# One layer of spiking attention and a mixture of experts: projections' inputs in four buffers, VectorE's work in a new order, biases in the first weight row, late weight pieces spread evenly

## The chip, the cores and the metric

The kernel runs on one core of a Trainium2 chip. The metric is device time in microseconds for one execution of the program. Five engines work side by side, each through its own instruction queue, and wait for each other on semaphores: TensorE (PE in the profile; its weight loads are PEld), VectorE (DVE), ScalarE (ACT), GpSimd (POOL) and SyncE (SP, which only issues DMAs). A DMA whose rows go to computed addresses (DMA_INDIRECT) is issued by GpSimd, one instruction for 128 rows.

## What is computed

The input x is (2, 2048, 256) float32, 4096 tokens. Cut to what matters:

```python
xn = (x - mean(x)) / sqrt(var(x) + 1e-5)                     # over the 256 features
Q, K, V = (spike(layer_norm(xn @ W.T + b) * g + beta - 1.0) for W, b, g, beta in q, k, v)
attn = Dh - hamming(Q, K) + log_pe_bias(N, N)                # 16 heads of 16; no softmax
out  = spike((attn * scale) @ V - 0.5)
out  = spike(layer_norm(out @ Wo.T + bo) * go + betao - 1.0)
gate = the two largest of softmax(xn @ router.T), scaled to sum 1    # 8 experts
moe  = sum over the two experts of gate * ((silu(h[:, :256]) * h[:, 256:]) @ down), h = xn @ up
result = x + out + moe
```

`spike(v)` is 1 where v >= 0, else 0. Since there is no softmax, attention is done as linear attention: a 16x16 sum of K-by-V products per head, and the position bias apart.

## The kernel before

**Tiles and stages.** Tokens go in 32 tiles of 128 (NT), tile t being block t // 2 of batch t % 2. Five stages follow each other, with engines overlapping at the seams.

1. *Start (0 to 49 us).* SyncE loads x in five chunks (`X_CHUNKS`), ScalarE's queue loads the four projection weights `w_f` and small tables. VectorE takes statistics (L760), GpSimd the power -1/2 (`first_rstd`, L648), VectorE normalises each tile in place (L782). TensorE transposes tiles (L1122), ScalarE copies them to `xT` (`keep_xT`), and TensorE forms the router's logits from them (L1134). The projection weights are centred over their output features and given the sign of the gain: ScalarE sums them (`sum_weights`, L418), VectorE subtracts and multiplies (L803). The biases take the same way on two partitions (L424, L807, L435, L813) into `bias_r`. ScalarE then rounds the weights to the fp32r type (`w_h`, L430) and VectorE keeps the rest (`w_l`, L818).
2. *Routing (50 to 65 us).* VectorE picks the two experts of each token and computes each row's slot, ending in `pos` (L896, semaphore `placed`). A second part, `rest_of_routing`, gives the slots of the padding rows (`pads_placed`) and the expert of each slot tile (`owner`).
3. *Projections (49 to 165 us).* For each tile ScalarE writes the rounded `xT_h` (`keep_xh`, L441) and VectorE the rest `xT_l` (`keep_xl`, L790), both in **two** buffers, so that tile t's must wait for the projections of tile t-2. TensorE computes Q, K and V of tile t: for each, one matmul of ones by `bias_r` (L1180), then for each of two chunks of features three products, high by high, high by low, low by high (L1102 to L1104). The results of two tiles (a pair) fill six half banks of PSUM; there are two such sets. ScalarE sums squares (`squares`, L494), takes the root (L500); VectorE refines it (`deviations`, L938 to L944), compares (`spikes`, L955), which frees the banks. TensorE turns Q of tile t-4 before tile t (L1168, one bank, emptied by ScalarE's `keep_qT`, L482), and adds K by V of tile t-4 after it (L1189). In the same stage the 24 pieces of expert weights are split into two fp32r parts: the first 8 by ScalarE and GpSimd (L453, L653), 16 later ones by ScalarE and VectorE (L453, L932), one for every second tile up to tile 19, then one a tile up to tile 27 (`late_piece`). Also in this stage GpSimd scatters the normalised rows to their slots in HBM (`slot_x`): 64 scatters of tiles (L672) and 7 of padding rows (L679, two behind each tile from tile 3 on). They start at `placed`; tile t's wait for all projections of tile t+2 (`proj_done` >= 3(t + LEAD)).
4. *Experts (175 to 373 us).* For each of 71 slot tiles: load `ex` from `slot_x`, transpose, up-projection, SiLU times the other half, transpose, down-projection, scatter to `slot_y`. SyncE issues the first load only when all 71 scatters have landed and all weight pieces are split (L349 to L351).
5. *Output (373 to 451 us).* Attention, output projection, gating, sums, store.

**What sets the order.** There is no planner: each engine's queue holds its instructions in the order in which its block of the code writes them, all 32 tiles written out. ScalarE's turn for tile t is: `keep_qT(t-4)`, `keep_xh(t+1)`, a late piece, then the squares. VectorE's is: `keep_xl(t+1)`; for even t `deviations` and three spikes of the pair before, for odd t its other three; then a late piece.

## Time and profile before

| | us |
|---|---|
| median of 3 runs | 454.08 (453.01 to 455.45) |
| the profiled execution, its own time | 452.64 |
| its span, first to last instruction | 450.8 |
| busy: TensorE / VectorE / ScalarE / GpSimd | 383.5 / 273.9 / 232.0 / 215.8 |
| mean granted TensorE clock | 0.941 of full speed |

A row of the timeline gives the start in us, the time in us, engine, line, operation, what is written and read, the count, and in brackets how long the engine was idle before it and who ended that. Where several like instructions stand in one row they overlap in the pipeline, so the distance between starts, not the mean time, is the price of one. A row of groups gives the busy time and the mean in ns, then the idle time before these instructions and its releasers. Idle time of an engine that is not the bottleneck costs nothing.

### The profile page before, as it was taken

What the parts mean: (1) busy time and instruction counts of PE and PEld (TensorE: products, weight loads), DVE (VectorE), ACT (ScalarE), POOL (GpSimd) and SP (SyncE); (2) the same over time, 40 slices, a digit from 0 to 9 for tenths busy, and PEclk for the clock granted to TensorE, in tenths of its full rate; (3) what the DMA queues carried; (4) which work ended last, traced back from release to release, by engine and by line L of the source; (5) the groups of instructions that cost most, each with busy time, mean ns of one, the idle gap of its engine ahead of it and who ended that gap; (6) DMA issues with size and microseconds to landing.
All of it is one profiled execution on the core that took longest, in us unless ns stands there. A gap on an engine that the chain in (4) does not pass through costs nothing.

```text
span 450.8 us, 8962 instructions
## 1 busy us (share of the span) xinstructions
PE 383.5 (85%) x2525; PEld 311.6 (69%) x2526; DVE 273.9 (61%) x774; ACT 232.0 (51%) x752; POOL 215.8 (48%) x213
## 2 busy tenths in 40 slices
PE   5489768688989944999999999999999998999860
PEld 1223758578988843788888888888888875666650
DVE  5799998346878733445444555445444534479984
ACT  1466745447687742444544545454545434566650
POOL 5252447666677671133333333333333332489983
PEclk9699889889999985899999999999999999999966
DMA  8752113334445322254443434343434323982222
GB/s 259 246 164 71 47 60 105 120 117 131 130 133 185 107 94 84 64 186 121 140 124 120 125 117 128 117 126 118 125 120 122 92 77 100 386 320 95 94 72 93
DMA packets 40434, 59.01 MB, mean 131 GB/s; under 512 B 6294, under 2 KB 27926, under 8 KB 40408
## 3 DMA queue, kind: packets, MB, share of 16 engines
q1 hardware_dynamic: 31712, 38.53, 28.5%
q0 software_dynamic: 6848, 18.70, 11.4%
q10 hardware_dynamic: 1848, 1.47, 1.1%
q8 instruction: 13, 0.21, 0.2%
q14 instruction: 13, 0.11, 0.1%
HBM read 35.79 MB, written 22.89 MB: 130 GB/s over the span
## 4 chain that ended last, share of the span: by engine, by line
PE 57%; DVE 12%; POOL 10%; issue 9%; ACT 5%; DMA 4%; SPq 1%; another core or an unknown queue 0%; POOLq 0%; DVEq 0%; ACTq 0%
PE bank L1104 15%; PE bank L1102 15%; PE bank L1103 14%; POOL xres L713 4%; PE bank L1228 3%; PE bank L1244 3%; POOL xres L706 3%; DMA xn<-x 3%; PE bank L1180 2%; DVE xn L782 2%; ACT junk L494 2%; DVE xst L760 2%; POOL slot_x L672 1%; POOL rstd L698 1%; DVE xT_l L790 1%
## 5 line engine op out<-in xcount | busy, mean ns | idle before, releaser
L687 POOL DMA_INDIRECT slot_y<-ey,dest x71 | 68.6, 966 | 138.2 <-ACT ey L547 108.4
L672 POOL DMA_INDIRECT slot_x<-xn,pos x64 | 66.4, 1038 | 34.9 <-PE bank L1104 15.2
L990 DVE TENSOR_TENSOR hid<-gact,bank 128x256 f32<-128x256 f32 x71 | 29.9, 421 | 78.2 <-ACT gact L531 52.4
L1102 PE MATMUL bank<-ew,exT_h 128*128 x142 | 63.6, 448 | 5.3 <-issue 4.5
L531 ACT ACTIVATE gact<-bank 128x256 f32<-128x256 f32 x71 | 27.4, 386 | 65.7 <-PE bank L1104 65.7
L1104 PE MATMUL bank<-ew,exT_l 128*128 x142 | 56.8, 400 | 0.0
L1103 PE MATMUL bank<-ew,exT_h 128*128 x142 | 56.8, 400 | 0.0
L1103 PE MATMUL bank<-w_l,xT_h 128*128 128x256 f32 x192 | 55.6, 290 | 1.3 <-issue 1.3
L1104 PE MATMUL bank<-w_h,xT_l 128*128 128x256 f32 x192 | 55.6, 290 | 0.2 <-issue 0.2
L1102 PE MATMUL bank<-w_h,xT_h 128*128 128x256 f32 x192 | 55.5, 289 | 0.1
L494 ACT ACTIVATE junk<-bank 128x256 bf16<-128x256 f32 x96 | 35.8, 384 | 37.2 <-PE bank L1104 37.2
L1102 PE MATMUL bank<-ew,hidT_h 128*128 x142 | 45.6, 321 | 1.0 <-DVE hidT_l L994 1.0
L541 ACT ACTIVATE hidT_h<-bank 128x256 fp32r<-128x256 f32 x71 | 27.3, 385 | 33.0 <-issue 23.0
L994 DVE TENSOR_TENSOR hidT_l<-bank,hidT_h 128x256 fp32r<-128x256 f32 x71 | 30.1, 424 | 21.0 <-ACT hidT_h L541 21.0
L1103 PE MATMUL bank<-ew,hidT_h 128*128 x142 | 39.9, 281 | 0.0
L1104 PE MATMUL bank<-ew,hidT_l 128*128 x142 | 39.9, 281 | 0.0
L1103 PEld LDWEIGHTS bank<-w_l,xT_h 128*128 128x128 f32 x192 | 38.2, 199 | 2.0 <-issue 2.0
L1180 PE MATMUL bank<-bias_r,ones_r 128*128 128x256 f32 x96 | 30.6, 318 | 10.2 <-DVE v_spk L955 4.9
L1102 PEld LDWEIGHTS bank<-w_h,xT_h 128*128 128x128 f32 x192 | 38.6, 201 | 0.0
L1104 PEld LDWEIGHTS bank<-w_h,xT_l 128*128 128x128 f32 x192 | 38.3, 199 | 0.4 <-issue 0.4
L924 DVE TENSOR_TENSOR exT_l<-bank,exT_h 128x256 fp32r<-128x256 f32 x71 | 29.6, 417 | 13.6 <-ACT exT_h L536 13.5
L1228 PE MATMUL bank<-id_f,ex 128*128 128x128 f32 x142 | 27.9, 280 | 9.6 <-DMA ex<-slot_x 9.5
(193 smaller groups left out, 960.9 us busy)
## 6 DMA issues: line engine op xcount, KB each, us to landing
ex<-slot_x SPq DMA_DIRECT2D x71, 129.0 KB
y_tok<-slot_y SPq DMA_DIRECT2D x8, 1024.0 KB, 13.9
ew_f<-experts SPq DMA_DIRECT2D x24, 256.0 KB
xres<-x SPq DMA_DIRECT2D x16, 256.0 KB
out<-xres SPq DMA_DIRECT2D x16, 256.0 KB, 2.1
xn<-x SPq DMA_DIRECT2D x6, 512.0 KB, 11.7
slot_y<-ey,dest POOLq DMA_INDIRECT x71, 2.4
xn<-x SPq DMA_DIRECT2D x4, 256.0 KB, 3.9
```

The costliest lines, as they stand in the source:

```text
L494: nc.scalar.activation(junk[:, i, :], proj_ps[r][i], ACT.Square, accum_out=ssq[:, r, i:i + 1]).then_inc(s["ssq_done"], 1)
L531: nc.scalar.activation(gact[:, m % 2, :], h_ps[m % 2][:, 0:F], ACT.Silu).then_inc(s["gact_done"], 1)
L672: pool.indirect_dma_start(slot_x, bass.IndirectOffsetOnAxis(ap=pos[:, k, t:t + 1], axis=0), xn[:, t, :], None).then_inc(s["scattered"], 16)
L687: pool.indirect_dma_start(slot_y, bass.IndirectOffsetOnAxis(ap=dest[:, m % 4:m % 4 + 1], axis=0), ey[:, m % 4, :], None).then_inc(y_out[m ...
L924: v.tensor_tensor(flat2(exT_l[:, m % 2, :, :]), ex_ps[m % 2], flat2(exT_h[:, m % 2, :, :]).bitcast(F32), ALU.subtract).then_inc(s["exl_set ...
L990: v.tensor_tensor(hid[:, m % 2, :], gact[:, m % 2, :], h_ps[m % 2][:, F:2 * F], ALU.mult).then_inc(s["hid_done"], 1)
L994: v.tensor_tensor(flat2(hidT_l[:, m % 2, :, :]), hT_ps[m % 2], flat2(hidT_h[:, m % 2, :, :]).bitcast(F32), ALU.subtract).then_inc(s["hidl_ ...
L1102: mm(dst, a_h, b_h, start=first, stop=False)
L1103: mm(dst, a_h, b_l, start=False, stop=False)
L1104: return mm(dst, a_l, b_h, start=False, stop=last)
L1180: mm(proj_ps[r][i], ones_r[:, :], bias_r[:, cols], start=True, stop=False)
L1228: last = turn(ex_ps[m % 2][:, c * P:(c + 1) * P], ex[:, u, c * P:(c + 1) * P], id_f[:, :])
```

## The change

**Biases.** A normalised row sums to zero over its 256 features, so subtracting the first row of a weight matrix from all its rows leaves the product as it is and makes the first row zero. The host now puts the biases of Q, K and V into that first row and passes the old one as `w_first`. The kernel loads it to all partitions (`w0_r`, 128 times 3 KB), GpSimd subtracts it from both chunks of `w_f` (`subtract_base`) and sets the first feature of every tile in `xT` to 1.0 after the router has read it (`set_ones`). The bias matmul L1180 goes from the projections (`bias_r` remains for the output projection alone, so the four bias steps work on a quarter of the data, or run once in place of four times). ScalarE's `sum_weights` moves behind its first two copies of `xT`, since it needs the subtracted weights.

**Buffers and order.** `xT_h` and `xT_l` have four buffers (`RING`). ScalarE's turn for tile t becomes: two squares first, then `keep_qT(t-4)`, `keep_xh(t+3)`, a late piece; for odd t the last two squares, the root and `keep_xh(t+3)` come behind. VectorE goes by pairs: `deviations`, `keep_xl`, four spikes, `keep_xl`, two spikes, then late pieces; `rest_of_routing` stands behind pair 1. TensorE waits for spikes bank by bank instead of once a tile.

**Late pieces.** The 16 late pieces go to tiles 5, 6, 8, 10, 11, 13, ... 28, 30, three to five tiles. Waits for piece buffers that hold older data are put at the piece concerned.

The diff, without renamed arguments and without the waits just named:

```diff
--- before.py
+++ after.py
+RING = 4
 ...
-        bias_r = keep("bias_r", [P, G4 * D], F32R)
+        bias_r = keep("bias_r", [P, D], F32R)
 ...
+        w0_r = place_in(r_a + KC * G3 * D * 4)("w0_r", [P, G3 * D])
 ...
-        xT_h = put("xT_h", [P, 2, KC, P], F32R)
-        xT_l = put("xT_l", [P, 2, KC, P], F32R)
+        xT_h = put("xT_h", [P, RING, KC, P], F32R)
+        xT_l = put("xT_l", [P, RING, KC, P], F32R)
 ...
-        def late_piece(m, i):
-            if m < 8 + LOOP and m % 2 == 0:
-                return None
-            n = POOL_PIECES + (m - PIECE_STEP) // 2 if m < 8 + LOOP else POOL_PIECES + (8 + LOOP - PIECE_STEP) // 2 + m - 8 - LOOP + 1
-            return (n + (0 if i is None else i * 2), n) if m >= PIECE_STEP and n < PIECES else None
+        LATE_PIECES = {PIECE_STEP + (n - POOL_PIECES) * 5 // 3: n for n in range(POOL_PIECES, PIECES)}
 ...
             act.dma_start(w_f[:, :, :], w_all.rearrange("(c k) n -> k c n", k=P)).then_inc(s["w_in"], 16)
+            act.dma_start(w0_r[:, :], w_first.partition_broadcast(P)).then_inc(s["base_in"], 16)
 ...
-                act.wait_ge(s["b_signed"], G4)
+                act.wait_ge(s["b_signed"], 1)
 ...
-            def keep_xh(t, m=None):
-                m = t if m is None else m
-                if not early(t, 2):
-                    act.wait_ge(s["proj_done"], G3 * (t - 1))
-                nc.scalar.activation(flat2(xT_h[:, m % 2, :, :]), xT_of(t), ACT.Copy).then_inc(s["xh_set"], 1)
 ...
-            act.wait_ge(s["w_in"], 16)
-            for n in range(KC * G4):
-                sum_weights(n)
             for g in range(NT // RG):
                 keep_xT(2 * g)
                 keep_xT(2 * g + 1)
+                if g == 0:
+                    act.wait_ge(s["w_based"], KC)
+                    for n in range(KC * G4):
+                        sum_weights(n)
 ...
-            def project(t, m, i):
-                if not early(t, 4):
-                    keep_qT(t - 4, m - 4)
-                if not (num(t) and t >= NT - 1):
-                    keep_xh(t + 1, m + 1)
-                late = late_piece(m, i)
-                if m == 11:
-                    act.wait_ge(s["bias_set"], 1)
-                    act.wait_ge(s["pads_done"], 16 * PC)
-                if late:
-                    piece_upper(late[0], late[1], i)
-                if m == 0:
-                    nc.scalar.activation(rstd[:, 0, 0:1], eps_c[:, 0:1], ACT.Sqrt)
-                if early(t, 4):
+            def project(t):
+                even = t % 2 == 0
+                if even:
+                    act.wait_ge(s["b_summed"] if t == 0 else s["ssq_done"], 1 if t == 0 else G3 * t)
+                act.wait_ge(s["proj_done"], G3 * t + (2 if even else 1))
+                squares(t, 0 if even else 2)
+                if t >= 4:
+                    keep_qT(t - 4, t - 4)
+                if even and t + 3 < NT:
+                    keep_xh(t + 3)
+                if t in LATE_PIECES:
+                    piece_upper(LATE_PIECES[t])
+                if t < 4:
                     for n in ((4, 5), (), (6, 7), ())[t]:
-                        piece_upper(n, n)
-                squares(t, m)
-                if m % 2 == 1:
-                    deviations(t, m)
+                        piece_upper(n)
+                if not even:
+                    act.wait_ge(s["proj_done"], G3 * t + 3)
+                    squares(t, 4)
+                    deviations(t)
+                    if t + 3 < NT:
+                        keep_xh(t + 3)
             act.wait_ge(s["eps_set"], 1)
             act.wait_ge(s["xT_ready"], NT // 2)
-            steps(project)
+            nc.scalar.activation(rstd[:, 0, 0:1], eps_c[:, 0:1], ACT.Sqrt)
+            keep_xh(1)
+            keep_xh(2)
+            for t in range(NT):
+                project(t)
 ...
-            for c in range(len(X_CHUNKS) - 1):
+            def subtract_base(c):
+                g.tensor_tensor(w_f[:, c, 0:G3 * D], w_f[:, c, 0:G3 * D], w0_r[:, :], ALU.subtract).then_inc(s["w_based"], 1)
+            def set_ones(group):
+                pool.wait_ge(s["logitsT"], group + 1)
+                n = RG if (group + 1) * RG <= XT_TILES else RG // 2
+                for t in range(0, RG, n):
+                    where, at = xT_part(group * RG + t)
+                    last = g.memset(where[0:1, at:at + n, 0, :], 1.0)
+                last.then_inc(s["ones_in"], 1)
+            first_rstd(0)
+            first_rstd(1)
+            pool.wait_ge(s["w_in"], 16)
+            pool.wait_ge(s["base_in"], 16)
+            subtract_base(1)
+            pool.wait_ge(s["w_based"], 1)
+            g.memset(w0_r[0:1, :], 0.0).then_inc(s["row0_gone"], 1)
+            pool.wait_ge(s["row0_gone"], 1)
+            subtract_base(0)
+            for c in range(2, len(X_CHUNKS) - 1):
                 first_rstd(c)
             piece_lower(0, 0)
             first_rstd(len(X_CHUNKS) - 1)
             for n in range(1, POOL_PIECES):
+                if n < 4:
+                    set_ones(n - 1)
                 if n == 4:
+                    for group in range(3, NT // RG):
+                        set_ones(group)
                     pool.wait_ge(s["w_halved"], 2 * KC)
                     g.tensor_tensor(wo_l[:, :, :], w_f[:, :, G3 * D:], wo_h[:, :, :].bitcast(F32), ALU.subtract).then_inc(s["wo_parted"], 1)
                 piece_lower(n, n)
 ...
-            def keep_xl(t, m):
+            def keep_xl(t):
                 dve.wait_ge(s["xh_set"], t + 1)
-                if not early(t, 2):
-                    dve.wait_ge(s["proj_done"], G3 * (t - 1))
-                v.tensor_tensor(flat2(xT_l[:, m % 2, :, :]), xT_of(t), flat2(xT_h[:, m % 2, :, :]).bitcast(F32),
+                if t >= RING:
+                    dve.wait_ge(s["proj_done"], G3 * (t - RING + 1))
+                v.tensor_tensor(flat2(xT_l[:, t % RING, :, :]), xT_of(t), flat2(xT_h[:, t % RING, :, :]).bitcast(F32),
                                 ALU.subtract).then_inc(s["xl_set"], 1)
 ...
-            for g in range(G4):
-                cols = bias_f[:, g * D:(g + 1) * D]
-                v.scalar_tensor_tensor(cols, cols, b_mean[:, 1, g:g + 1], sgn_r[0:2, g * D:(g + 1) * D],
-                                       ALU.subtract, ALU.mult).then_inc(s["b_signed"], 1)
-            keep_xl(0, 0)
+            v.scalar_tensor_tensor(bias_f[:, :], bias_f[:, :], b_mean[:, 1, 0:1], sgn_r[0:2, G3 * D:],
+                                   ALU.subtract, ALU.mult).then_inc(s["b_signed"], 1)
+            keep_xl(0)
 ...
-            def project(t, m, i):
-                pair = (t // 2 if num(t) else i * 2 + m // 2) - 1
-                if not (num(t) and t >= NT - 1):
-                    keep_xl(t + 1, m + 1)
-                if m % 2 == 0:
-                    deviations(t - 2, m - 2, pair)
-                    spikes(t - 2, m - 2, 0)
-                else:
-                    spikes(t - 3, m - 3, 1)
-                late = late_piece(m, i)
-                if late:
-                    piece_lower(*late)
+            def project(pair):
+                deviations(pair)
+                keep_xl(2 * pair + 4)
+                spikes(pair, 0, 4)
+                keep_xl(2 * pair + 5)
+                spikes(pair, 4, 6)
+                if pair == 0:
+                    dve.wait_ge(s["bias_set"], 1)
+                if pair == 1:
+                    rest_of_routing()
+                for t in (2 * pair + 2, 2 * pair + 3):
+                    if t in LATE_PIECES:
+                        piece_lower(LATE_PIECES[t], LATE_PIECES[t])
             dve.wait_ge(s["w_parted"], KC)
             dve.wait_ge(s["wo_parted"], 1)
-            deviations(0, 0, 0)
-            spikes(0, 0, 0)
-            keep_xl(4, 4)
-            spikes(0, 0, 1)
-            dve.wait_ge(s["bias_set"], 1)
-            def later_project(t, m, i):
-                if not early(t, 4):
-                    project(t, m, i)
-                if m == 4:
-                    rest_of_routing()
-            steps(later_project)
+            for pair in range(NT // 2 - 2):
+                project(pair)
+            deviations(NT // 2 - 2)
+            spikes(NT // 2 - 2, 0, 6)
+            for t in (NT - 2, NT - 1):
+                if t in LATE_PIECES:
+                    piece_lower(LATE_PIECES[t], LATE_PIECES[t])
 ...
-            def project(t, m):
-                r = m // 2 % 2
+            def project(t):
+                r = t // 2 % 2
                 pe.wait_ge(s["xl_set"], t + 1)
-                if not early(t, 4):
-                    pe.wait_ge(s["spk_done"], G3 * (t - 4) + 4 if m % 2 == 0 else G3 * (t - 4) + 3)
-                for i in range(m % 2 * G3, (m % 2 + 1) * G3):
+                for i in range(t % 2 * G3, (t % 2 + 1) * G3):
+                    if t >= 4 and i in (0, 2, 4):
+                        pe.wait_ge(s["spk_done"], 2 * G3 * (t // 2 - 2) + i + 2)
                     g = PAIR[i][1]
                     cols = slice(g * D, (g + 1) * D)
-                    mm(proj_ps[r][i], ones_r[:, :], bias_r[:, cols], start=True, stop=False)
                     for c in range(KC):
-                        last = three(proj_ps[r][i], xT_h[:, m % 2, c, :], xT_l[:, m % 2, c, :], w_h[:, c, cols], w_l[:, c, cols],
-                                     False, c == KC - 1)
+                        last = three(proj_ps[r][i], xT_h[:, t % RING, c, :], xT_l[:, t % RING, c, :], w_h[:, c, cols], w_l[:, c, cols],
+                                     c == 0, c == KC - 1)
                     last.then_inc(s["proj_done"], 1)
 ...
+    w_first = w_all[0, 0:G3 * D].copy()
+    w_all[0, 0:G3 * D] = np.concatenate([w("attn_b" + n) for n in "qkv"])
```

## Rows read from the trace of the kernel before

**Rows 1.** Chain of waits, from 160 us: start us, us, what.

```profile
161.25 0.96 POOL slot_x L672
...
170.10 2.59 DMA slot_x<-xn,pos
172.71 2.03 DMA ex<-slot_x
...
174.79 0.70 PE bank L1228 x2
```

**Rows 2.** Groups of the whole span: count | busy, mean ns | idle before.

```profile
L672 POOL DMA_INDIRECT slot_x<-xn,pos x64 | 66.4, 1038 | 34.9 <-PE bank L1104 15.2 <-issue 14.9 <-DVE pos L896 4.7
...
L494 ACT ACTIVATE junk<-bank 128x256 bf16<-128x256 f32 x96 | 35.8, 384 | 37.2 <-PE bank L1104 37.2
L1180 PE MATMUL bank<-bias_r,ones_r 128*128 128x256 f32 x96 | 30.6, 318 | 10.2 <-DVE v_spk L955 4.9 <-DVE xT_l L790 3.2 <-issue 1.7
...
L679 POOL DMA_INDIRECT slot_x<-pad_rows,pad_i x7 | 6.7, 961 | 2.1 <-issue 2.1
...
L807 DVE SCALAR_TENSOR_TENSOR bias_f<-bias_f,b_mean,sgn_r 2x256 f32<-2x256 f32 x4 | 1.7, 466 | 0.0
...
L435 ACT ACTIVATE bias_h<-bias_f 2x1024 fp32r<-2x1024 f32 x1 | 1.1, 1057 | 2.0 <-DVE bias_f L807 2.0
...
L638 POOL MEMSET bias_r<- 128x1024 f32 x1 | 1.0, 961 | 0.0
```

**Rows 3.** GpSimd's timeline (columns told above).

```profile
18.91 1.74 POOL L648 TENSOR_TENSOR xrstd<-xvar,neg_half 128x8 f32<-128x8 f32 x1 [6.88 <-DVE xvar L774]
...
32.88 1.28 POOL L653 TENSOR_TENSOR ew<-ew_f,ew 128x512 fp32r<-128x512 f32 x1
...
65.61 1.06 POOL L672 DMA_INDIRECT slot_x<-xn,pos  x1 [4.70 <-DVE pos L896]
...
102.94 0.96 POOL L672 DMA_INDIRECT slot_x<-xn,pos  x1 [1.37 <-PE bank L1104]
...
109.08 1.19 POOL L672 DMA_INDIRECT slot_x<-xn,pos  x1 [1.40 <-PE bank L1104]
...
133.26 1.47 POOL L672 DMA_INDIRECT slot_x<-xn,pos  x1 [0.30 <-issue]
```

**Rows 4.** TensorE's timeline: tile 4's start, then a seam of two tiles.

```profile
68.07 0.36 PE L1180 MATMUL bank<-bias_r,ones_r 128*128 128x256 f32 x1 [0.53 <-DVE v_spk L955]
...
77.43 0.28 PE L1189 MATMUL bank<-v_spk,qk_spk 128*128 128x128 bf16 x2
...
77.63 0.36 PE L1180 MATMUL bank<-bias_r,ones_r 128*128 128x256 f32 x1
77.83 0.28 PE L1102 MATMUL bank<-w_h,xT_h 128*128 128x256 f32 x1
77.95 0.28 PE L1103 MATMUL bank<-w_l,xT_h 128*128 128x256 f32 x1
```

**Rows 5.** VectorE's timeline.

```profile
15.00 2.71 DVE L760 BATCH_NORM_STATS2 xst<-xn 128x6 f32<-128x256 f32 x8 [3.01 <-DMA xn<-x]
...
23.78 2.66 DVE L782 TENSOR_SCALAR xn<-xn,xmean,xrstd 128x256 f32<-128x256 f32 x8
...
31.01 7.16 DVE L782 TENSOR_SCALAR xn<-xn,xmean,xrstd 128x256 f32<-128x256 f32 x16
...
47.94 0.96 DVE L818 TENSOR_TENSOR w_l<-w_f,w_h 128x768 fp32r<-128x768 f32 x1 [0.42 <-ACT wo_h L431]
...
133.22 0.68 DVE L932 TENSOR_TENSOR ew<-ew_f,ew 128x512 fp32r<-128x512 f32 x1
```

**Rows 6.** Two stretches: busy us (count) of each engine, TensorE clock, DMA share, GB/s.

```profile
0.00:15.00 15.00, 6.91 (x24) 2.81 (x25) 7.10 (x39) 4.56 (x18) 7.32 (x16) 1.00 0.89 270
174.00:186.00 12.00, 9.89 (x40) 7.45 (x41) 6.58 (x20) 4.63 (x11) 0.00 (x0) 0.64 0.23 65
```

**Rows 7.** DMA issues: KB each, median us from issue to landing.

```profile
thr_r<-vec_d SPq DMA_DIRECT2D x1, 512.0 KB, 4.3
```

96 lines of the change are left out of this document (50 added, 46 removed).

## The prediction

> **What bounds the kernel now.** I read the engines' busy times first: TensorE leads with 383.5 of 450.8 us, and the change takes one of its groups away, the 96 bias matmuls of the projections (L1180), 30.6 us of busy time [rows 2]. Busy time is not yet time won, so the second view was the chain of waits. There the projection stage does not end in TensorE. From 161.25 us the chain is GpSimd's: eight scatters back to back, the last from 170.10, then 2.6 us until it has landed, 2.0 us for the first load, and the experts start at 174.79 [rows 1]. TensorE's projections are over soon after 161 and it waits.
>
> So the question is what sets the scatters. GpSimd's groups show 64 scatters with 66.4 us busy and 34.9 us of idle time before them: 15.2 us in 14 waits for projections, 14.9 us in 49 gaps of its own (0.30 each), 4.7 us for the slots; and 7 pad scatters with 6.7 us [rows 2]. The first starts at 65.61, when routing is done [rows 3]. The limit of this stage is therefore a sum of two things: when routing ends, and 71 scatters plus what TensorE makes them wait.
>
> **The floor of the scatters.** 66.4 + 6.7 = 73.1 us, plus 70 gaps of 0.30 = 21.3, from 65.61: 160.0. Measured, the last ends at 170.10 + 0.96 = 171.06 (the length that an undisturbed scatter has in rows 3). So 11.0 us at most come from removing all waits for projections. Everything that TensorE wins beyond that ends in a longer wait for the scatters.
>
> **Do the waits go?** The scatters at 102.94 and 109.08 are those of tiles 10 and 12 by their count, and waited for the ends of tiles 12 and 14, so a pair of tiles takes 6.14 us [rows 3]. A product starts every 0.118 us [rows 4]. A pair had 42 of them (4.96); without six for biases 36, 4.25 us. The turn of Q and the K by V sums cost 77.63 - 77.43 = 0.20 a tile and about 0.05 of semaphores, 0.5 a pair. That is 4.75. The rest before, 0.7 us a pair, is mostly waiting: for `xT_l` (two buffers: it could only be written after the tile before last) and for spikes, the 10.2 us in front of L1180 [rows 2]. Four buffers let `xT_h` and `xT_l` run up to three tiles ahead, so the first of the two goes. What is late next is ScalarE's `keep_qT`: it now stands behind two squares that wait for TensorE's second group; two squares at some 0.37 and a copy at 0.3 make 1.1 us after that group, against 0.71 + 0.25 that TensorE has left in the tile, so perhaps 0.15 us a tile is waited. I take 5.2 us a pair. Bounds: 4.75, and 6.5 if ScalarE falls behind.
>
> Must that be reached? TensorE's tile 4 starts at 68.07 [rows 4]. The last gate of the scatters is the end of tile 30, 13.5 pairs later. The last eight scatters start 171.06 - 161.25 = 9.8 us before the end, so without loss at 160.7 - 9.8 = 150.9. That allows (150.9 - 68.1) / 13.5 = 6.13 us a pair. At 5.2 us TensorE is there at 138.3, 12.6 us early. Even before, the steady pace nearly met that; what cost the waits was the early part: tile 12 was done at 102.9, 34.8 us after 68.1, where 4.5 pairs at 6.14 take 27.6, that is 7.2 us of stalls. With either the pace or the stalls gone the scatters hardly wait. Left over are the first gates (tiles 4 and 5, which GpSimd meets at once after routing, and `pads_placed`, now behind six spikes and two `keep_xl` of pair 1): I take 0.7 us, bounds 0 and 3.
>
> **Scatters beside VectorE.** A scatter takes 0.96 us undisturbed; at 133.26 one took 1.47 with `piece_lower` starting at 133.22 [rows 3, 5]. In all, the 71 carry 73.1 - 71 x 0.96 = 4.9 us of this. The change keeps the 16 pieces and 32 `keep_xl`, only at other moments, so I take no difference. Bounds: all collisions gone, -4.9; each of 16 pieces costing 0.51 and each of 28 `keep_xl`, shorter instructions of the same kind, an estimated 0.2, 13.8 us, that is +8.9. The Trainium skill (SBUF — State Buffer, section "Who interferes with whom") says that a VectorE instruction with two SBUF inputs contends with a GpSimd instruction that reads SBUF, and that the loser is blocked, not slowed. By that rule the sum depends on how many meet and not on how dense they are, the same zero; the trace agrees in that the 1.47 belongs to a scatter that began just behind such an instruction.
>
> **The start: when does routing end?** Three terms move the 65.61.
> - *Fewer bias steps.* VectorE's four subtractions (L807) were 1.7 us busy with a little overlap; three go, 1.2 us. ScalarE's `bias_h` falls from 1.06 us for 1024 columns to some 0.4, so 0.66 [rows 2]. Both lie in the chain, since VectorE waits for ScalarE's weights right after [rows 5]: -1.9. The smaller sums of biases and `bias_r` lie beside other work: nothing.
> - *One more load.* `w0_r` is 128 x 3 KB = 393 KB, in a stretch where DMA is 0.89 busy at 270 GB/s, and VectorE waits there for x until 15.00 with 3.01 us of idle time before it [rows 5, 6]. After that VectorE has no gap until the biases, so a delay there passes through whole. 393 / 270 = 1.46 us; part may come behind x, so +1.2 (0 to 1.5).
> - *GpSimd's new instructions.* A subtraction of 128x512 takes 1.28 us [rows 3], so the two of 128x768 take 1.9 each. They fall where VectorE waits or takes statistics. Cover gone, they would cost up to their 3.8. The eight `set_ones` write 512 elements of one partition: half of L638's 0.96, 0.48 each [rows 2], and most fall beside the last normalisations. Those show what a meeting costs: 8 in 2.66 us, but 16 in 7.16 with two `piece_lower` beside them, 1.84 too much, 0.9 for each [rows 5]. No row shows a fill beside VectorE: 0 to 8 x 0.48 = 3.8 us. I take 0.6, nearer to nothing because a fill is short and reads nothing. By the rule named above, a fill would block only VectorE instructions that use both port pairs; if the normalisation were one, the sum would be 3.2 us higher.
>
> ScalarE's `sum_weights` moves behind two copies and the subtractions. VectorE wants the sums only when its last normalisation ends, at 31.01 + 7.16 = 38.2 [rows 5], and the copies that they delay wait for those normalisations anyway: nothing. Were that cover gone, it would cost their some 3 us. Together -1.9 + 1.2 + 0.6 = -0.1.
>
> **After the scatters.** The 276.0 us from 174.79 to the end of the span [rows 1] run the same instructions. TensorE will now stand idle over 20 us before them instead of some 12, but its clock was already down: 0.64 granted in the first 12 us of the experts [rows 6]. A longer rest can't take more than that start; nothing. The late pieces end with tile 30's, well ahead of the last scatter.
>
> **Sum.** -11.0 + 0.7 - 0.1 = -10.4. The profiled execution took 452.64 us (1.84 around its span), so the same execution would be 442.2. It lies 1.4 below the median of the runs shown, 454.08; from that the forecast is **443.7**.
>
> **Rivals.**
> 1. *ScalarE's new order holds TensorE back.* At 6.5 us a pair tile 30 ends at 68.1 + 87.8 = 155.9, 5.0 us late: 448.7. For it: 96 squares carry 35.8 us plus their read-outs, and 37.2 us of waiting for TensorE stands before them [rows 2], which now becomes waiting for `keep_qT` behind it. Against: that waiting is also ScalarE's room.
> 2. *Nothing is won:* pace 6.14 and the 7.2 us of early stalls both stay, so the change doesn't do what it says; tile 30 ends where it did, 454. Against: the missing `xT_l` at several of the stalls.
> 3. *More is won:* the load hides behind x (-1.2), the fills cost nothing (-0.6), half the collisions go (-2.5): 439.4.
> 4. *Slower: `w0_r` comes late.* GpSimd's queue is in order, and `first_rstd` of the third chunk now stands behind the subtractions. Its result was used from 23.78 [rows 5]. Back from there: 1.74 for it [rows 3], 3.8 + 0.72 for the subtractions and the fill between, so `w0_r` must be there by 17.5; each us beyond holds VectorE's normalisation and all behind it. From 17.5 + 10.4 + 2.3 = 30.2 the kernel is slower than before by over 0.5%; at 33, 457. For it: it is a broadcast behind other loads of ScalarE's queue. Against: a broadcast of 512 KB landed in 4.3 us [rows 7].
>
> **How the numbers follow.** Forecast 0.72; rival 1 0.12; rival 2 0.04; rival 3 0.06; rival 4 0.06. Faster by over 0.5% (2.3 us, about what a measurement of this kernel can tell): forecast, rivals 1 and 3, 0.90. Within: rival 2, 0.04. Slower: rival 4, 0.06. The range starts at rival 3's 439.4 and reaches above rival 1's 448.7, which also holds the bounds of the waits (+2.3), the fills (+3.2) and a third of the collisions (+3), not all at once: 439.0 to 449.5.
>
> **What would show it.** Right: L1180 gone from the projections; waits of the scatters for TensorE under 3 us; first scatter at 63.5 to 67.5, last one starting at 159 to 161; experts 4.7 us later; 276 us from there to the end; TensorE finished with tile 31 before 145 and idle for 15 us or more. The step "do the waits go" is wrong if over 5 us of such waits stay, the start is wrong if the first scatter is off by over 2 us, and the collisions if the mean scatter leaves 0.98 to 1.09 us.

## The result: slower on the first chip, and the profile after

The changed kernel took 459.63 us median (457.15 to 462.01, 6 runs), the kernel before 454.56 beside it: ratio 1.0123, interval 1.0075 to 1.0171. Forecast were 443.7. The profiled execution took 462.01, its span 460.2. In one kernel below (chip D, the changed one with stops) four of six executions count as slow, over 1.5% above its fastest and at a lower granted clock, and are left out of what is concluded.

The groups of the whole span, and then the chain of waits, both of the changed kernel on that chip:

```profile
PE 374.9 (81%) x2421; PEld 303.6 (66%) x2430; DVE 275.7 (60%) x771; ACT 229.7 (50%) x746; POOL 221.9 (48%) x225
...
L690 POOL DMA_INDIRECT slot_x<-xn,pos x64 | 64.5, 1008 | 40.6 <-PE bank L1116 26.2
...
L484 ACT ACTIVATE junk<-bank 128x256 bf16<-128x256 f32 x96 | 36.0, 382 | 52.3 <-PE bank L1116 47.5
```

```profile
179.37 2.85 DMA slot_x<-xn,pos
...
182.24 2.05 DMA ex<-slot_x
...
184.33 0.70 PE bank L1238 x2
```

The bias matmuls of the projections are gone, yet TensorE is busy only 8.6 us less, for the 30.6 that they carried. The scatters wait 26.2 us for products (15.2 in [rows 2]), the last one starts at 179.37, 9.3 us later than in [rows 1], and from the experts' first matmul to the end it is 460.2 - 184.33 = 275.9 us, against 276.0 forecast. So in the two profiled executions the loss stands wholly ahead of the last scatter.

GpSimd's timeline at the start, with two of VectorE's rows, statistics of the second part of x and the last normalisations, in the second fence (columns: start us, us, engine, line, op, out<-in, count, and in brackets the idle time before it and what ended it):

```profile
13.43 1.80 POOL L651 TENSOR_TENSOR w_f<-w_f,w_r 128x768 f32<-128x768 f32 x1 [1.00 <-DMA w_r<-w_first]
...
16.10 1.81 POOL L651 TENSOR_TENSOR w_f<-w_f,w_r 128x768 f32<-128x768 f32 x1
20.31 1.74 POOL L643 TENSOR_TENSOR xrstd<-xvar,neg_half 128x8 f32<-128x8 f32 x1 [2.40 <-DVE xvar L792]
...
34.07 0.65 POOL L658 MEMSET xT<- 1x512 f32 x1
...
63.51 2.81 POOL L648 TENSOR_TENSOR ew<-ew_f,ew 128x512 fp32r<-128x512 f32 x2 [6.37 <-ACT ew L449]
66.66 1.06 POOL L690 DMA_INDIRECT slot_x<-xn,pos  x1 [0.34 <-DVE pos L912]
```

```profile
16.40 2.71 DVE L778 BATCH_NORM_STATS2 xst<-xn 128x6 f32<-128x256 f32 x8 [4.01 <-DMA xn<-x]
...
32.22 8.29 DVE L800 TENSOR_SCALAR xn<-xn,xmean,xrstd 128x256 f32<-128x256 f32 x16
```

The new load had landed by 13.43, far ahead of 17.5, and the third `first_rstd` still waited 2.40 us for VectorE: rival 4 did not happen. VectorE's statistics start at 16.40, though, where [rows 5] have 15.00: the x that they wait for came later. The first scatter is 1.05 us later than in [rows 3], where -0.1 was forecast.

TensorE's waits from 62 to 175 us, and those of GpSimd from 62 to 180 us in the second fence (columns: what waits and for what, us in total, times, longest):

```profile
PE bank L1180 <- ACT qT L478: 22.7, 11, 3.1
PE bank L1180 <- DVE v_spk L971: 3.4, 1, 3.4
```

```profile
POOL slot_x L690 <- PE bank L1116: 26.2, 19, 2.8
```

That is the new wait. Six more, 3.1 us in all, which the profile puts down to nothing ("issue"), end like these about 0.14 us after ScalarE's copy has ended. TensorE no longer waits for `xT_l`; it waits for ScalarE's copy of Q out of its one bank (`keep_qT`, L478), before it may turn the next Q there. Tile 4 starts, with its turn of Q, at 68.63 and tile 31's last product at 171.8: 14 pairs at 7.37 us. One such wait, in ScalarE's timeline and, in the second fence, in TensorE's:

```profile
131.64 0.40 ACT L436 ACTIVATE xT_h<-xT 128x256 fp32r<-128x256 f32 x1
134.33 0.39 ACT L484 ACTIVATE junk<-bank 128x256 bf16<-128x256 f32 x1 [2.30 <-PE bank L1116]
...
134.71 0.38 ACT L484 ACTIVATE junk<-bank 128x256 bf16<-128x256 f32 x1
...
135.06 0.38 ACT L478 ACTIVATE qT<-bank 128x256 bf16<-128x256 bf16 x1
```

```profile
131.91 0.28 PE L1116 MATMUL bank<-w_h,xT_l 128*128 128x256 f32 x1
...
132.70 0.28 PE L1199 MATMUL bank<-v_spk,qk_spk 128*128 128x128 bf16 x2
135.59 0.37 PE L1180 MATMUL bank<-id_b,qk_spk 128*128 128x128 bf16 x2 [2.60 <-ACT qT L478]
...
136.30 0.41 PE L1116 MATMUL bank<-w_h,xT_l 128*128 128x256 f32 x1
136.51 0.41 PE L1114 MATMUL bank<-w_h,xT_h 128*128 128x256 f32 x1
```

The squares at 134.33 need the tile's second group, whose last product starts at 131.91 and ends at 132.19. ScalarE was free at 132.04 and started 2.1 us after that end. What kept it is not in the trace: the profile names TensorE, which had long been done. The copy of Q is queued behind those squares, so TensorE starts again at 135.59, and then at the lower level of its clock (granted 0.50, 1.2 of 2.4 GHz, from 135.1 to 138.4), products 0.21 us apart instead of 0.118. From 66 to 176 us 77 products followed one another at that distance, 26 in the kernel before, the bias matmuls counted in; the difference at 0.095 us each is 4.8 us.

The kernel before has such stops too. Its ScalarE and then its TensorE, on the same chip:

```profile
121.64 0.41 ACT L441 ACTIVATE xT_h<-xT 128x256 fp32r<-128x256 f32 x1
124.07 0.39 ACT L494 ACTIVATE junk<-bank 128x256 bf16<-128x256 f32 x1 [2.02 <-PE bank L1104]
```

```profile
121.50 0.28 PE L1104 MATMUL bank<-w_h,xT_l 128*128 128x256 f32 x1
...
122.53 0.28 PE L1168 MATMUL bank<-id_b,qk_spk 128*128 128x128 bf16 x2
```

The same 2 us of ScalarE, but its `keep_qT` had run ahead of the stop, at 121.38, and TensorE turned the next Q at 122.53 with no wait (0.88 us of waiting for spikes came four microseconds later). One can count such stops without the profile's releasers: how long after both the awaited product and ScalarE's own last instruction had ended do the squares start? From 66 us on that is over 0.5 us in 15 places of the kernel before, 22.6 us together and up to 3.2, and in 11 places of the changed kernel, 25.0 us. So the stops are not the change's. TensorE's waits at a turn of Q that end just behind ScalarE's copy, whatever name the profile gives them, are 4.9 us before and 27.3 after, from 66 to 176 us.

### The profile page after: what moved, and what is told of

Same layout as the page of the kernel before. It is cut to its first block, busy times and chain, and to the rows that moved or that the text cites. A ratio compares the mean times of both kernels' runs of the same rounds, so it can differ in the third digit from the quotient of the medians.

```text
span 460.2 us, 8750 instructions
## 1 busy us (share of the span) xinstructions
PE 374.9 (81%) x2421; PEld 303.6 (66%) x2430; DVE 275.7 (60%) x771; ACT 229.7 (50%) x746; POOL 221.9 (48%) x225
## 4 chain that ended last, share of the span: by engine, by line
PE 59%; DVE 10%; POOL 9%; issue 9%; ACT 5%; DMA 5%; SPq 1%; POOLq 0%; DVEq 0%; ACTq 0%; another core or an unknown queue 0%
PE bank L1116 17%; PE bank L1114 17%; PE bank L1115 15%; POOL xres L731 4%; PE bank L1238 3%; PE bank L1254 3%; POOL xres L724 3%; DMA xn<-x 3%; ACT junk L484 2%; DVE xn L800 2%; DVE xst L778 2%; DMA ex<-slot_x 1%; PE bank L1180 1%; POOL rstd L716 1%; POOL slot_x L690 1%
## 5 line engine op out<-in xcount | busy, mean ns | idle before, releaser
L690 POOL DMA_INDIRECT slot_x<-xn,pos x64 | 64.5, 1008 | 40.6 <-PE bank L1116 26.2
L1114 PE MATMUL bank<-w_h,xT_h 128*128 128x256 f32 x192 | 61.4, 320 | 0.3 <-DVE w_l L834 0.3
L1115 PE MATMUL bank<-w_l,xT_h 128*128 128x256 f32 x192 | 58.9, 307 | 0.0
L1116 PE MATMUL bank<-w_h,xT_l 128*128 128x256 f32 x192 | 58.7, 306 | 0.0
L536 ACT ACTIVATE hidT_h<-bank 128x256 fp32r<-128x256 f32 x71 | 27.3, 385 | 33.2 <-issue 23.0
L1114 PEld LDWEIGHTS bank<-w_h,xT_h 128*128 128x128 f32 x192 | 41.6, 217 | 0.6 <-issue 0.4
L1116 PEld LDWEIGHTS bank<-w_h,xT_l 128*128 128x128 f32 x192 | 41.9, 218 | 0.0
L1115 PEld LDWEIGHTS bank<-w_l,xT_h 128*128 128x128 f32 x192 | 41.5, 216 | 0.0
L1114 PEld LDWEIGHTS bank<-ew,exT_h 128*128 128x128 f32 x142 | 27.1, 191 | 12.6 <-issue 9.6
```

Of the source, the lines that this page charges most:

```text
L536: nc.scalar.activation(flat2(hidT_h[:, m % 2, :, :]), hT_ps[m % 2], ACT.Copy).then_inc(s["hidh_set"], 1)
L690: pool.indirect_dma_start(slot_x, bass.IndirectOffsetOnAxis(ap=pos[:, k, t:t + 1], axis=0), xn[:, t, :], None).then_inc(s["scattered"], 16)
L1114: mm(dst, a_h, b_h, start=first, stop=False)
L1115: mm(dst, a_h, b_l, start=False, stop=False)
L1116: return mm(dst, a_l, b_h, start=False, stop=last)
```

## The experiments

The chips differ, so each ratio is to the kernel before on the same chip. (For the first comparison no chip number was kept; it may be one of the others, E for instance.) "Last" is the start of the last scatter in the profiled execution; the span ends 279 to 283 us after it in every profile of every kernel here, whatever was changed.

| chip | kernel | median us (before) | ratio, interval | last us |
|---|---|---|---|---|
| first | changed | 459.63 (454.56) | 1.0123, 1.0075 to 1.0171 | 179.4 |
| B | changed, copy of Q first | 442.26 (443.31) | 0.9982, 0.9948 to 1.0016 | 160.2 |
| B | before, copy of Q late | 449.37 | 1.0114, 1.0027 to 1.0201 | 167.6 |
| B | before, bias row alone | 440.23 | 0.9942, 0.9906 to 0.9979 | 157.6 |
| B | before, LEAD 0 | 439.93 | 0.9933, 0.9894 to 0.9973 | 157.2 |
| C | before, for its profile | 444.56, one run | | 163.2 |
| C | changed | 440.19 (443.51) | 0.9927, 0.9898 to 0.9957 | 158.9 |
| C | changed, copy of Q first | 441.54 | 0.9949, 0.9924 to 0.9974 | 160.5 |
| C | changed, filled | 443.8 | 0.9983, 0.9951 to 1.0015 | 161.4 |
| D | changed, stops | 442.11 and 446.15 (443.72); all six: 450.07 | 1.001 for those two, no interval | 160.3 |
| D | copy of Q first, stops | 441.64 | 0.9954, 0.9932 to 0.9976 | 159.3 |
| D | before, stops | 447.91 | 1.011, 1.0065 to 1.0154 | 164.6 |
| D | before, pads late | 441.31 | 0.9944, 0.9921 to 0.9967 | 161.0 |
| E | changed | 459.46 (454.92) | 1.0104, 1.0049 to 1.0158 | 176.7 |
| E | changed, stops | 467.95 | 1.0269, 1.0195 to 1.0342 | 184.2 |
| E | before, three edits | 454.26 | 0.9988, 0.9955 to 1.002 | 170.9 |
| E | copy of Q first, LEAD 0 | 454.68 | 0.9987, 0.9952 to 1.0022 | 172.1 |
| F | changed | 441.01 (442.91) | 0.9956, 0.9926 to 0.9986 | 158.0 |
| F | changed, copy of Q first | 442.6 | 0.9989, 0.9963 to 1.0014 | 158.9 |

**The order of the copy alone, both ways (chip B).** In the changed kernel, and the reverse in the kernel before:

```diff
 def project(t):                 # changed kernel
-    act.wait_ge(s["proj_done"], G3 * t + (2 if even else 1))
-    squares(t, 0 if even else 2)
     if t >= 4:
         keep_qT(t - 4, t - 4)
+    act.wait_ge(s["proj_done"], G3 * t + (2 if even else 1))
+    squares(t, 0 if even else 2)
```

```diff
 def squares(t, m):              # kernel before, behind each tile's first two squares
+    if i in (1, 3) and t >= 4:
+        keep_qT(t - 4, m - 4)
 def project(t, m, i):
-    if not early(t, 4):
-        keep_qT(t - 4, m - 4)
```

> The changed kernel with one thing moved: ScalarE's copy of the turned Q (keep_qT of tile t-4) stands first in its turn for tile t again, ahead of the two squares. Theory 1 (the copy behind the squares holds TensorE at each turn of Q): TensorE's 22.7 us of waits for that copy fall under 4, the scatters' waits for projections from 26.2 to under 5, the last scatter starts at 160 to 163, and the time is 443 to 448. Theory 2 (without the bias matmuls TensorE has too little work between its waits to keep its clock, whatever the order): the clock in the projections stays at 0.83 in half of its stretches and the time at 455 or more. Theory 3 (the late pieces in their new places hold VectorE, and so the banks): waits for spikes take the place of those for the copy, 452 or more.

> The kernel before with that one thing alone: keep_qT of tile t-4 behind the first two squares of tile t (for odd t too). Theory 1: TensorE waits 1 us or more at most turns of Q, a pair of tiles takes 7 us or more instead of 6.14, the last scatter starts 5 to 12 us later and the time is 458 to 466. Theories 2 and 3 expect no difference beyond 1 us: 453 to 456.

With the copy first, tile 31 was through at 135.6, 4.85 us a pair, and the last scatter started at 160.20. But this chip has none of the first one's stops, and the changed kernel itself was not run on it, so this does not show that the order made the first chip's loss. The kernel before lost 1.1% by that edit alone (four runs), less than expected: its pair takes 6.67 us and not 7 or more, and no wait but the longest is over 1.3. TensorE's waits for Q in it, from 66 to 176 us:

```profile
PE bank L1168 <- ACT qT L482: 11.8, 15, 4.6
```

The longest is the wait for the pads, told below; the kernel before has 7.3 us of such waits on chip C, so the edit brought some 4.5.

**Parts alone (chip B).** The biases in the first weight row with all that belongs to it, and `LEAD = 3` made `LEAD = 0`, by which a scatter waits for its own tile's products and not for those three tiles on.

> The kernel before with the biases in the first weight row alone; two buffers, the order of all engines and the late pieces as before. Theory 1: no harm in this part; the pair takes some 5.5 us, the scatters wait under 6 us for projections instead of 15.2, last one at 161 to 166, time 445 to 450. Theory 2: the clock falls more often in the projections and the time is 456 or more. For the start: first scatter at 65 to 67, as the 66.66 of the changed kernel.

> The kernel before with the scatters of tile t gated by the projections of tile t-1 and not t+2 (LEAD 0 in place of 3). If 71 scatters back to back are the floor that the prediction took, the first starts at 65.6, the last at 158.5 to 160.5, and the experts start when TensorE's last tiles end or at 163.5, whichever is later: time 443 to 449. If scatters slow each other or the projections when nothing spreads them, their mean rises over 1.1 us, or TensorE's waits grow, and the time is over 451.

Both end the scatters' waits for products, and both then stop at the same place: first scatter 65.19 and 65.01, last 157.56 and 157.21. 71.8 us of scatters less the last, and 21.0 of gaps, from 65.01 give 156.9. The floor of the forecast is there; both came out faster than expected.

**The changed kernel again, and with TensorE kept busy (chip C).** Was the first chip's loss the lower clock of a TensorE with less work? The filled kernel has one more matmul, overwritten by the next, ahead of each group:

```diff
 for i in range(t % 2 * G3, (t % 2 + 1) * G3):
+    mm(proj_ps[r][i], ones_r[:, :], wo_h[:, 0, :], start=True, stop=True)
```

> The changed kernel, unchanged, beside the others. Theory 1 (TensorE waits for keep_qT behind the squares) has two parts: a steady one of 0.5 us a pair where ScalarE's chain between two turns is longer than a tile, and one of 2.6 us wherever ScalarE itself stops for some 2.2 us. On a chip where ScalarE stops rarely only the first is left: TensorE's waits for the copy at 5 to 10 us and the time at 444 to 450, within 1% of before. Where it stops often as in the first profile: 1% slower than before again.

> The changed kernel with one matmul more in front of each projection, of the shape of the bias matmul that went, whose product is overwritten: it computes nothing that is used. It gives TensorE its old load back. Theory 2 (the clock falls since TensorE has too little work): the clock recovers and the time falls to that of before or under. Theory 1: TensorE's waits for the copy get shorter by what the fill takes, 0.35 us a tile, and its own work longer by as much; the time is that of the changed kernel within 3 us, above or below.

> The changed kernel with keep_qT ahead of the squares, again, for the same chip as the changed kernel. Theory 1: faster than the changed kernel by its scatters' waits less 5 us, the first load of the experts at 162 to 164 on any chip, 442 to 445. Theory 2 (clock without bias matmuls): no faster than the changed kernel.

> The kernel before, unchanged, for a profile on the chip of these comparisons: the runs of before were 454 us beside the change and 443 us beside the four experiments so far, whose parts from the last scatter to the end all take 280 us as in the first profile. If the two chips differ in the projections alone, this profile has the last scatter at 160 to 163 where the time is 443, or at 170 where it is 454.

Here the changed kernel is faster, and the fill only costs: 0.9983, 3.6 us more than the changed kernel, somewhat beyond the 3 expected. But there is no loss to explain on this chip: 8 products of the changed kernel stand 0.21 us apart, 10 of the filled one. Whether want of work lowers the clock on a chip with stops was not tried, so that rival stands. ScalarE's squares never start over 0.5 us late on this chip. What is left of the wait is its steady part, once in a pair; TensorE's waits from 66 to 176 us, a seam of its timeline, and ScalarE's copy in the third fence:

```profile
PE bank L1180 <- ACT qT L478: 8.9, 15, 1.3
```

```profile
131.47 0.28 PE L1199 MATMUL bank<-v_spk,qk_spk 128*128 128x128 bf16 x2
132.30 0.27 PE L1180 MATMUL bank<-id_b,qk_spk 128*128 128x128 bf16 x2 [0.55 <-ACT qT L478]
```

```profile
131.04 0.38 ACT L484 ACTIVATE junk<-bank 128x256 bf16<-128x256 f32 x1
...
131.77 0.38 ACT L478 ACTIVATE qT<-bank 128x256 bf16<-128x256 bf16 x1
```

Pair 5.46 us (77.70 to 83.15 and on, at each such seam), against 5.2 forecast; the wait came 0.55 a pair where 0.15 a tile was written. It costs nothing there: last scatter 158.89, waits beyond the gaps about 1 us. The copy of Q first, expected to be faster than the changed kernel, is 1.35 us slower by the medians here and 1.6 on chip F.

**Stops put in on purpose (chip D).** Six more copies, 1.93 us together, just before the squares of five tiles, in three kernels:

```diff
+    if t in (6, 12, 16, 22, 26):
+        for k in range(6):
+            nc.scalar.activation(junk[:, k, :], wo_h[:, 0, :].bitcast(F32), ACT.Copy).then_inc(s["stopped"], 1)
+        act.wait_ge(s["stopped"], 6 * ((6, 12, 16, 22, 26).index(t) + 1))
```

> The changed kernel with six more copies of ScalarE (some 0.3 us each, about 2 us together) just ahead of the squares of tiles 6, 12, 16, 22 and 26, to imitate the stops of ScalarE of 2.2 us that the first profile of the changed kernel shows at such places. Theory (the copy of Q out of the one bank stands behind the squares, so a stop of ScalarE passes whole into TensorE): five waits of TensorE for that copy of 2 to 3 us, products 0.21 us apart behind each, last scatter at 163 to 172 us, ratio to before 1.00 to 1.02. Rival (the stops are hidden by the scatters' floor, and the first chip was slow for another reason): last scatter at 159 to 160.5, ratio 0.99 to 0.995.

> The same extra copies in the changed kernel with the copy of Q ahead of the squares. Theory: TensorE waits less than 1 us for the copy at each stop, since the copy is out before ScalarE stops; last scatter at 160 to 162, ratio 0.995 to 1.00. Rival: squares that come 2 us later hold the projections' banks or VectorE as well, and TensorE waits the same sum under another name: last scatter as in the kernel with the copy behind.

> The same extra copies in the kernel before, behind its copy of Q and ahead of its squares. Theory: the old order hides each in part, its waits of TensorE for the projections' inputs stay what they are; last scatter 162 to 166, ratio 1.00 to 1.01, so the changed kernel loses 5 us or more to the stops and the kernel before less than 3. Rival: all three kernels lose the same 4 to 8 us.

In the changed kernel's profile four of the five pass whole into a wait for Q, of 2.3 us each; at tile 6 TensorE waits 2.28 for spikes. ScalarE, TensorE and its waits from 62 to 182 us:

```profile
93.72 1.93 ACT L498 ACTIVATE junk<-wo_h 128x256 bf16<-128x256 f32 x6
...
96.41 0.38 ACT L478 ACTIVATE qT<-bank 128x256 bf16<-128x256 bf16 x1
```

```profile
96.94 0.27 PE L1184 MATMUL bank<-id_b,qk_spk 128*128 128x128 bf16 x2 [2.27 <-ACT qT L478]
```

```profile
PE bank L1184 <- ACT qT L478: 15.4, 14, 2.3
```

and with the copy of Q first, ScalarE and TensorE's waits:

```profile
90.91 0.36 ACT L478 ACTIVATE qT<-bank 128x256 bf16<-128x256 bf16 x1
91.17 1.94 ACT L500 ACTIVATE junk<-wo_h 128x256 bf16<-128x256 f32 x6
```

```profile
PE bank L1184 <- ACT qT L478: 3.8, 6, 1.3
```

So with the copy first TensorE pays less for such stops, but not nothing: its last product starts at 153.5 with the copy late and at 141.2 with it first, where the same kernels without stops have 145.3 and 135.9 on chip C. The five stops add 8.1 and 5.3 us. In time the difference is not shown. The two executions of the former that count took 442.11 and 446.15, against a median of 441.64; the profiled one is the 442.11. With its waits of 2.3 us and hardly any slow products (13) its last scatter still started at 160.34, where 163 to 172 were expected: the stops were hidden by the scatters' floor, as the rival had it. The other four took 449.7 to 452.42, at a granted clock of 0.928 to 0.936 for 0.953, and no profile shows what they lost. The kernel before lost 4.2 us, more than the 3 expected.

**The wait for the pads (chip D).** The kernel before has ScalarE wait at tile 11 until the pads are scattered; its row on chip C, and TensorE's waits there from 66 to 176 us:

```profile
96.99 0.63 ACT L453 ACTIVATE ew<-ew_f 128x512 fp32r<-128x512 f32 x1 [7.77 <-issue]
```

```profile
PE bank L1168 <- ACT qT L482: 7.3, 2, 6.0
```

On the first chip the wait cost nothing: ScalarE came to tile 11 so late that the pads had landed, and its piece followed at once. The piece's row, in the kernel before on that chip:

```profile
100.23 0.62 ACT L453 ACTIVATE ew<-ew_f 128x512 fp32r<-128x512 f32 x1
```

The change moved that wait to piece 15. Done alone:

```diff
 def piece_upper(n, m, i):
+    if n == BIAS_PIECE:
+        act.wait_ge(s["bias_set"], 1)
+    if n == PAD_PIECE:
+        act.wait_ge(s["pads_done"], 16 * PC)
 def project(t, m, i):
-    if m == 11:
-        act.wait_ge(s["bias_set"], 1)
-        act.wait_ge(s["pads_done"], 16 * PC)
```

> The kernel before with nothing but ScalarE's wait for the pads of the slots moved from tile 11 to the piece that carries them (piece 15; the wait for the biases to piece 13), as the change has it. Theory: the wait of 6 us of TensorE for the copy of Q near 97 to 100 us goes, the lead that it took is kept, and the scatters no longer wait: last scatter at 158 to 160.5, ratio 0.990 to 0.997. Rival (the lead was enough even with that wait, or a later wait takes its place): last scatter at 161 to 163, ratio 0.998 to 1.002.

0.9944, about the whole gain of the changed kernel where it gains. (Its profile is of the slowest execution of eleven, 445.22, hence the last scatter at 161.0.) TensorE's waits for Q in it, from 66 to 176 us, are 5.3 us fewer than on chip C:

```profile
PE bank L1169 <- ACT qT L486: 2.0, 2, 1.3
```

**Further chips (E and F).**

> The changed kernel as it is, on a further chip. If the loss of the first chip is that of ScalarE's stops, which two of three chips did not show: ratio 0.990 to 0.997, no stop of ScalarE above 1 us ahead of the squares, last scatter at 158 to 160. If this chip has the stops: ratio 1.00 to 1.02 and last scatter at 165 to 180.

> The changed kernel with the five imitated stops of ScalarE again. Theory (a wait of 2.3 us of TensorE lets its clock fall, which costs as much again): in an execution of 447 to 452 us the trace has the five waits of 2.3 us and more than 80 products 0.21 us apart, and the scatters wait more than 6 us for TensorE; in one of 442 it has fewer than 60. Rival (the time is lost elsewhere, as in the experts): last scatter at 160 to 161 in an execution of 447 to 452 us too.

> The kernel before with three edits that each brought 0.6 to 0.7% alone: the biases in the first weight row, ScalarE's wait for the pads at piece 15, LEAD 0. Floor theory (each alone already takes nearly all of the scatters' waits for TensorE away): together they give no more than the best alone, last scatter at 157 to 158.5, ratio 0.989 to 0.995. Rival (they add up): last scatter below 156, ratio 0.980 to 0.988.

> The changed kernel with the copy of Q ahead of the squares and LEAD 0 (positions and spikes of a tile come three tiles sooner among its steps). Floor theory: first scatter 1 us sooner, none waits for TensorE, last at 158 to 160, ratio 0.990 to 0.996. Rival (VectorE's new order and LEAD 0 stand in each other's way, since spikes come before the statistics they need): TensorE waits for v_spk, last scatter at 162 or later, ratio 1.00 or more.

> The changed kernel with the copy of Q ahead of the squares, beside the changed kernel as it is on the same chip. Theory: on a chip where before takes 452 us or more and engines stop for nothing that the profile shows, ratio 0.995 to 1.003, 1% below the changed kernel's; on one of 442 to 446 us without stops, ratio 0.993 to 0.999 and within 0.4% of the changed kernel's. Rival (LEAD 0 made the difference): on a chip with stops the same ratio as the changed kernel's, 1.007 to 1.013.

> The changed kernel as it is. Theory: ratio 1.007 to 1.015 on a chip with stops of ScalarE (before at 452 us or more), 0.990 to 0.997 on one without (before at 442 to 446 us). A ratio on the other side of 1 than the chip's time says would refute it.

Chip E is like the first: before at 454.92, the changed kernel 1.0% slower, and stops. The changed kernel's rows there, for ScalarE, TensorE and GpSimd in turn:

```profile
92.99 0.38 ACT L484 ACTIVATE junk<-bank 128x256 bf16<-128x256 f32 x1 [5.83 <-remote]
```

```profile
94.25 0.37 PE L1180 MATMUL bank<-id_b,qk_spk 128*128 128x128 bf16 x2 [8.36 <-ACT qT L478]
```

```profile
93.25 0.96 POOL L690 DMA_INDIRECT slot_x<-xn,pos  x1 [2.32 <-remote]
```

A stop of 5.83 us of ScalarE became 8.36 us of TensorE; its waits for Q sum to 24.2 us and the scatters' for products to 24.1, the first chip's 22.7 and 26.2 again. ScalarE's squares start over 0.5 us late in eight places, 20.8 us together. The stops put in on top cost 8.5 us (467.95 against 459.46): last scatter at 184.19 for 176.68, 79 slow products for 43. That they lower the clock by themselves this does not show, since the chip's own stops are mixed in. On chip F, which has none, the changed kernel won 0.4%.

The two other kernels of chip E were level with before, although both were expected to be faster, with the last scatter at 157 to 160 where it started at 170.9 and 172.1. That speaks against the order of the copy as what saves them. In the kernel with the copy first and LEAD 0 TensorE waits as long for Q as in the changed kernel, 28.0 us for 27.5 from 66 to 176 us. The profile puts most of it down to nothing, but ScalarE's copy has just ended each time, and was itself late. ScalarE's row and TensorE's:

```profile
94.41 0.39 ACT L478 ACTIVATE qT<-bank 128x256 bf16<-128x256 bf16 x1 [3.54 <-remote]
```

```profile
94.94 0.37 PE L1180 MATMUL bank<-id_b,qk_spk 128*128 128x128 bf16 x2 [10.97 <-issue]
```

Its tile 31 ends at 171.0, no earlier than the changed kernel's 169.4. The kernel before with three edits, which has the old order of all engines, ends it at 171.8, with 13.4 us of waits for Q. What the two share is no bias matmul and LEAD 0, whose scatters wait for products three tiles sooner. The two kernels that differ in the order alone met chip F, where there are no stops. No version beat both kernels on all chips; of those tried, the ones with the copy first or with LEAD 0 were not slower than before, and the copy first was 0.3 to 0.4% slower than the changed kernel on chips C and F, which have no stops.

## Why the prediction was wrong

*The floor of the scatters: right.* The last one starts at 158.0 to 160.5 in the kernels of the change on chips B, C and F (161.4 in the filled one), for 159 to 161 forecast; time = last scatter + 280 held in all profiles. With no waits more was not to be had.

*The sum, on chips like C: right in kind, too big.* The kernel before waited less there (last scatter 163.2 against 170.1), so at the same floor it moves by 4.3 us and the medians by 3.3, and not 10.4. The pace of 6.79 us a pair on the first chip was 6.39 on chip C. The waits that I read in one profile were in part that chip's stops, and such a part I took for something the change removes. That holds for the "7.2 us of stalls" ahead of tile 12 too: squares of tiles 6 to 9 started 0.7 to 3.2 us late. On chip C the stall there is another, ScalarE's wait for the pads at tile 11, which the first chip's trace does not have.

*The step that failed: "perhaps 0.15 us a tile is waited" for `keep_qT`.* That is rival 1's mechanism with a larger price: TensorE waited 22.7 us for the copy in 11 waits, 27.3 with those of other names, and a pair took 7.37 us where 5.2 was taken. Steadily it is 0.55 us a pair, 5.46 a pair with it, harmless against 6.13 allowed (6.09, in fact: the last gate is tile 31's end with six scatters behind it, not tile 30's with eight). But I summed ScalarE's work as if it began when TensorE's group ended. On the first chip ScalarE was late again and again, by up to 3.2 us, also in the trace of before, where I could have read it: a wait of 2.02 us "for TensorE" with the awaited product over since 121.8. Behind the squares the copy passes such a stop on whole (2.6 us of TensorE for 2.15 of ScalarE, 8.36 for 5.83), and products came 0.21 us apart behind it. That the old order would have spared the changed kernel this is not shown: on chip E the copy first had the same waits. 7.37 us a pair is above even the bound of 6.5, and what is above 6.09 goes into the end: 14 x 1.28 = 17.9; the scatters' waits beyond their gaps measured 21.2.

*Rival 4: refuted.* Landed by 13.43 against 17.5 needed. (By the rival's own sum 33 gives 459, not 457.)

*The start: 1.1 us off, by a term that I had not.* The load cost about what was forecast: VectorE's statistics of the second part of x start at 15.04 to 16.41 in the 14 profiles with it, at 14.45 to 15.37 in the six without, 1.0 us apart in the mean. The fills cost too: the last 16 normalisations take 8.29 us, against 7.16 in [rows 5], with the same two pieces beside them and three fills, at most 0.4 each where one fill is 0.65 long. So a fill seems to hold VectorE, which by the Trainium skill (SBUF — State Buffer, section "Who interferes with whom") it does only where the VectorE instruction uses both port pairs; the fills alone were not tried. All that and the saved bias steps cancel, as forecast: the biases alone start their first scatter at 65.19, between the 65.01 and 65.69 of the two other kernels on chip B with the old start. What is left comes from the new order. ScalarE hands over its last pieces of the start later, and GpSimd starts its halves of them at 62.0 to 63.5 in the kernels with the new order, 55.8 to 58.5 in the others. The scatters stand behind them in GpSimd's queue. On chip C VectorE had the positions at 64.90, against 64.84 before, and GpSimd was not free until 66.09:

```profile
63.43 2.66 POOL L648 TENSOR_TENSOR ew<-ew_f,ew 128x512 fp32r<-128x512 f32 x2 [6.71 <-ACT ew L449]
66.26 1.06 POOL L690 DMA_INDIRECT slot_x<-xn,pos  x1 [0.17 <-issue]
```

On the first chip positions and pieces were ready at about the same time (66.3); there one of VectorE's instructions for the positions (L907) took 1.51 us beside those pieces where its neighbour took 0.42.

*Collisions: right.* A mean scatter took 1.008 us, inside 0.98 to 1.09, and 71 of them 71.2 us for 73.1.

*After the scatters: right,* 275.9 for 276.0. TensorE rested 8.72 us before, not over 20; after a rest of 16.24 on chip C the end comes 280.9 behind the last scatter, on the first chip 280.8.

*What stays open.* Why ScalarE stops on some chips; and why the changed kernel loses 1% there. For the order of the copy speak: the waits for Q of 27.3 us where before had 4.9, the one-line edit that cost before 1.1%, and the put-in stops, which add 8.1 us to TensorE's end behind the late copy and 5.3 behind the early one. Against it speaks that the copy first had the same waits on chip E, and that a kernel with the old order but without the bias matmuls finished its projections as late there. So a rival stands: in the kernel before the bias matmuls and the waits for inputs gave ScalarE room for its stops, and whatever takes that room away brings them to TensorE. No kernel with the order alone ran on a chip with stops.

## What to carry to other kernels

Where a copy frees the only buffer of another engine, look at what stands ahead of it in its queue: behind work that waits for that engine it cost half a microsecond a pair here, and most put-in stops passed on whole. Another floor hid that here, and moving the copy ahead won no time. Before removing a wait, ask what its room may be hiding, and look in the trace for an engine that starts late after the thing it waits for was over. And where a stage has a floor, reckon from it on more than one chip: a forecast of "waits removed" is worth only what this chip has of them.

## What of the hardware was not expected

- The same kernel takes 442.9 to 443.7 us on four chips, 454.9 on chip E and 454.6 on the first (perhaps the same one). In the six profiles of those, ScalarE stops for a cause that the profile does not name: its squares start over 0.5 us late in 8 to 15 places, 18.8 to 31.2 us in a stage of 110, up to 7.88 us at once. GpSimd had one stop of 2.32 us, TensorE some of up to 1.75 between its matmuls. In the 14 profiles of the other four chips no square starts over 0.5 us late.
- Idle time that the profile gives to "issue" can be a plain wait. TensorE's 10.97 us on chip E end 0.14 us after ScalarE's copy, like its named waits.
- Behind a wait of TensorE of 2.6 us the products came 0.21 us apart, at the lower clock, for some while; behind a wait of 2.27 us on chip D they came 0.12 apart at once, at a granted clock of 1.00 (13 slow ones in the whole stage). The length of a wait alone doesn't say it.
- Fills of one partition, 512 elements, took 0.65 us beside VectorE's normalisations and 0.52 later, beside none of them.
